# Four residual graph layers: edge counts by windows of 125 keys, with the first head's projection between the windows

## The reference

```
h = relu(layernorm(x));  x = x + GAT(h)    # layer 0 and 1: 4 heads of 512, elu, then 1 head of 768
h = relu(layernorm(x));  x = x + RGCN(h)   # layer 2: three convolutions over 3 relations
h = relu(layernorm(x));  x = x + GAT(h)    # layer 3: 8 heads of 96, elu, then 1 head of 768

GAT:  hW = h @ W                                     # per head
      e  = leaky_relu(as[src] + ad[dst], 0.2)        # for each edge, and for each node's loop to itself
      alpha = exp(e - max over the target's edges) / (their sum + 1e-16)
      out[dst] += alpha * hW[src];   out + b
RGCN: xw = h @ w_rel[r];  inv[dst, r] = 1 / (number of edges of type r into dst), 0 where there are none
      out[dst] += xw[edge_type, src] * inv[dst, edge_type];   out + h @ w_root + b;  relu
```

## Time and profile before

| | us |
|---|---|
| median of 3 runs | 1873.45 |
| lowest and highest | 1873.04, 1873.78 |
| the profiled execution | 1874.38 |
| its span | 1872.6 |
| PE, DVE, ACT, POOL busy | 1575.7, 880.6, 579.8, 517.1 |

### The profile page before, as it was taken

The page is one execution under the profiler, slowest core; times in us unless marked ns, Lnnn a source line. Parts: engine busy times, 40 slices in busy tenths (PEclk is TensorE's granted clock), DMA queues, the critical chain, the costliest instruction groups (busy, mean ns, idle before and its releaser), DMA issues.

```text
span 1872.6 us, 27057 instructions
## 1 busy us (share of the span) xinstructions
PE 1575.7 (84%) x10264; PEld 1515.3 (81%) x10264; DVE 880.6 (47%) x2103; ACT 579.8 (31%) x1165; POOL 517.1 (28%) x671
## 2 busy tenths in 40 slices
PE   3978888997779889976899999999999995566777
PEld 2647888896779888976899999999999995556777
DVE  4995566423356664233634223140322134678633
ACT  2114444332244343222231222322221222355421
POOL 1014233332242233313222332323232222222121
PEclk7998898997889899988899999999999997767797
DMA  1112111122221111223111122112122222100012
GB/s 50 38 37 69 45 46 45 35 67 77 66 64 33 40 46 34 80 69 110 39 39 42 50 64 64 54 49 62 49 68 82 75 85 71 38 1 1 5 47 86
DMA packets 85290, 99.24 MB, mean 53 GB/s; under 512 B 8742, under 2 KB 77788, under 8 KB 85166
## 3 DMA queue, kind: packets, MB, share of 16 engines
q1 hardware_dynamic: 68660, 66.50, 12.4%
q10 hardware_dynamic: 16506, 31.07, 5.1%
HBM read 85.76 MB, written 11.77 MB: 52 GB/s over the span
## 4 chain that ended last, share of the span: by engine, by line
PE 61%; DVE 11%; issue 10%; ACT 7%; DMA 6%; POOL 3%; DVEq 1%; ACTq 0%; POOLq 0%; SPq 0%
PE ps L705 35%; PE ps L768 7%; PE ps L871 6%; PE ps L853 4%; PE ps L735 3%; DMA xl<-x_scratch 2%; PE ps L830 2%; DVE prob L1693 2%; DVE junk L1646 2%; DMA xl<-in_x 1%; PE ps L892 1%; POOL pairs L966 1%; PE ps L915 1%; ACT pairs L1049 1%; DVE rl L1729 1%
## 5 line engine op out<-in xcount | busy, mean ns | idle before, releaser
L966 POOL TENSOR_TENSOR pairs<-stage,pairs 128x256 fp32r<-128x256 f32 (+3 forms) x472 | 370.0, 802 | 792.7 <-ACT pairs L1049 791.5
L705 PE MATMUL ps<-pairs,XB 128*125 128x256 f32 (+2 forms) x2880 | 416.4, 307 | 28.1 <-POOL pairs L966 17.0
L705 PEld LDWEIGHTS ps<-pairs,XB 128*125 128x125 f32 (+1 forms) x2880 | 409.5, 195 | 31.7 <-issue 18.0
L705 PE MATMUL ps<-pairs,XA 128*125 128x256 f32 (+3 forms) x2655 | 375.2, 303 | 1.1 <-DVE Hl L1354 1.1
L705 PEld LDWEIGHTS ps<-pairs,XA 128*125 128x125 f32 (+2 forms) x2655 | 370.6, 189 | 2.8 <-DVE Hl L1354 1.7
L1049 ACT ACTIVATE pairs<-stage 128x256 fp32r<-128x256 f32 (+3 forms) x472 | 188.9, 424 | 554.7 <-PE ps L705 426.4
L768 PE MATMUL ps<-AT,Hg 125*128 125x314 f32 (+1 forms) x1080 | 167.4, 316 | 15.3 <-ACT full L1107 7.9
L768 PEld LDWEIGHTS ps<-AT,Hg 125*128 125x128 f32 (+1 forms) x1080 | 161.8, 191 | 17.3 <-ACT full L1107 9.2
L1354 DVE TENSOR_TENSOR Hl<-ps,Hl 125x768 fp32r<-125x768 f32 (+3 forms) x57 | 43.6, 818 | 273.0 <-ACT Hl L1099 273.0
L735 PE MATMUL ps<-ident,prob 125*125 125x125 f32 x475 | 89.9, 348 | 82.3 <-ACT full L1107 35.6
L735 PEld LDWEIGHTS ps<-ident,prob 125*125 125x125 f32 x475 | 80.5, 254 | 88.3 <-issue 34.2
(11 more groups left out here) (196 smaller groups left out, 1706.3 us busy)
## 6 DMA issues: line engine op xcount, KB each, us to landing
stage<-in_W SPq DMA_DIRECT2D x192, 128.0 KB, 2.3
stage<-in_rel SPq DMA_DIRECT2D x99, 192.0 KB, 2.4
stage<-in_root SPq DMA_DIRECT2D x91, 64.0 KB, 1.8
x_scratch<-xo ACTq DMA_DIRECT2D x15, 375.0 KB
xl<-x_scratch ACTq DMA_DIRECT2D x15, 375.0 KB
stage<-in_rel SPq DMA_DIRECT2D x42, 128.0 KB, 2.1
stage<-in_root SPq DMA_DIRECT2D x12, 192.0 KB, 2.4
stage<-in_W SPq DMA_DIRECT2D x12, 192.0 KB, 2.4
```

The source lines that it names most:

```text
L705: last = mm(o, X[:rows, xi, a, P * (s0 + t):P * (s0 + t) + m], pair(n, b), start=k == 0 and i == 0 and t * pitch % BANK == 0, stop=k == le ...
L966: nc.gpsimd.tensor_tensor(pair(n, 1), staged(n), pair(n, 0).bitcast(F32), ALU.subtract).then_inc(*up("weights_lo", "weights lo", n))
```

## The change

In neutral words, part by part:

1. **Windows.** The key on the target side is now 3 x target + type, and the source alone the key on the other side. 1875 target keys make 15 windows of 125 (`NW`, `KW`). A chunk now costs a `srcs` of 626 keys and a `dsts` of 125, and 2 products of 313 columns into 2 banks. A group is 2 chunks (`EG` = 2), with 2 pairs of one-hot buffers. With these edges the 15 windows take 3, 4, 3, 4, 4, 4, 3, 4, 3, 4, 4, 3, 4, 4 and 3 passes: 54, so 108 chunks.
2. **The start.** `bounds` works on 16 windows and 40 groups: 32 transposes on PE and 15 additions in a row on DVE instead of 10 and 5, two reductions that must see both halves, and two more small operations. PE and DVE load their trip counts with one address load and 32, 31 register loads. All five `load_x` stand before all five `norm_T`.
3. **Regrouping.** A window's counts are one ACT copy (with one row sum), and SP writes them to DRAM. After every third window SP waits for the writes and reads 125 x 1875 counts back as `cr_back`, one row for each target. DVE's `sum_relations` works on that, and has 4 operations instead of 7; the absent pairs are found by POOL, the logarithm with the loops to itself by ACT in two operations (`log_self`).
4. **Order.** Behind each of the windows 0 to 11 stands one weight tile of head 0's projection (15 products); the rows of chunk 0 are copied at window 5, those of chunk 1 at window 11, the dots stand at windows 7 and 13, and the `graph` steps at windows 4, 7, 10, 13 and behind 14.
5. **Degrees and repeats.** The row sums stand as 125 x 15, are transposed by PE (`degree_T`), written to DRAM and read back as `cnt`. The `repeats` step stands behind the dots of head 1's first chunk.
6. **SP** loads weights only as far as the splits of the steps that it has passed.

```diff
-EG = 4
+EG = 2
+KW = 125
+NW = R * N // KW
+NB = 16
+SP2 = N + 1
...
     if l == 0:
-        yield ("repeats",)
...
+        for w in range(NW):
+            yield ("count", w)
+            if w < 12:
+                yield ("part", chunk(0, w // 6), w % 6, w % 6 + 1)
+                yield ("split", chunk(0, w // 6), w % 6 + 1)
+            if w in (5, 11):
+                yield ("rows", chunk(0, w // 6))
+            if w in (7, 13):
+                yield ("dots", chunk(0, w // 6 - 1 if w == 7 else 1))
+            if w % 3 == 1 and w > 3:
+                yield ("graph", w // 3 - 1)
+        yield ("graph", NT - 1)
...
             yield second
+            if l == 0 and h < 0:
+                yield ("degree_T",)
+                yield ("repeats",)
+            if l == 0 and h == 0:
+                yield ("inverse",)
...
-    for d in range(NT + 2):
-        if d < NT:
-            yield ("load_x", d)
-        if d > 1:
-            yield ("norm_T", 0, d - 2)
+    yield ("split", ("project", 0, 0, 256), 0)
     for d in range(NT):
-        yield ("count", d)
+        yield ("load_x", d)
+    for d in range(NT):
+        yield ("norm_T", 0, d)
...
-                    q = acquire(*s, banks=4)
-                    o = ps[:P, place[q] * BANK:(place[q] + 4) * BANK]
-                    for c in range(4):
-                        last = mm(o[:, BANK * c:BANK * c + BANK], zero16[:, :P], zero16[:, :], start=True,
+                    w = s[1]
+                    q = acquire(*s)
+                    o = halves(q, P, SP2 // 2)
+                    for c in range(2):
+                        last = mm(o[:, c, :], zero16[:, :P], zero16[:, :SP2 // 2], start=True,
...
+                            for c in range(2):
+                                last = mm(o[:, c, :], dsts[:, i, :KW],
+                                          srcs[:, i, SP2 // 2 * c:SP2 // 2 * c + SP2 // 2],
                                           start=False, stop=True, skip_group_check=True)
...
+                    sp.dma_start(cr_scr[KW * w:KW * w + KW, :], cr[:, w % 2, :N]).then_inc(
+                        *up(f"counts_out{w % 2}", "counts out", w, by=16))
+                    if w % 3 == 2:
+                        d = w // 3
+                        sp.wait_ge(*at("counts out", w))
+                        sp.wait_ge(*at("counts out", w - 1))
+                        sp.dma_start(cr_back[:, d, :].rearrange("p (r n) -> p r n", r=R),
+                                     cr_scr[R * P * d:R * P * d + R * P, :].rearrange("(p r) n -> p r n", r=R)).then_inc(
+                            *up(f"counts_back{d}", "counts back", d, by=16))
...
-                    load_weights(LOADS)
-                elif s in tiles_of:
-                    load_weights(wend[s] + 12)
+                parted = max(parted, split_limit(s))
+                load_weights(next((n for n in range(len(W)) if (stage_before[n] or 0) >= max(parted, 1)), len(W)))
...
+                elif kind == "graph":
+                    d = s[1]
+                    pool.wait_ge(*at("edge counts", d))
+                    nc.gpsimd.tensor_scalar(lnc[:, d, :N], cn[:, d % 2, :N], 0.0, ABSENT, ALU.is_equal,
+                                            ALU.mult).then_inc(*up("pool_step", "absent", False, d))
...
+                    log_mask(False, d, cw, 1 - d % 2)
...
-                    for d in range(NT):
-                        step(V.tensor_tensor(span[:, 2, d + 1:d + 2], span[:, 2, d:d + 1], span[:, 1, d:d + 1],
+                    for w in range(NW):
+                        step(V.tensor_tensor(span[:, 2, w + 1:w + 2], span[:, 2, w:w + 1], span[:, 1, w:w + 1],
                                              ALU.add))
...
-                            V.tensor_scalar(srcs[:, i, :], iota16[:P, :], edgef[:, 0, bass.ds(group * EG + i, 1)],
+                            V.tensor_scalar(srcs[:, i, :], iota16[:P, :SP2], edgef[:, 0, bass.ds(group * EG + i, 1)],
...
-                dve.wait_ge(*at("relation counts", d))
+                dve.wait_ge(*at("counts back", d))
                 if d >= 2:
                     dve.wait_ge(*at("graph out", d - 2))
+                    dve.wait_ge(*at("mask", False, d - 2))
```

More of the change, by code:

```diff
@@ L924, in _ @@
         def _(sp):
-            loaded = [0]
+            loaded, parted = [0], 0
             def load_weights(upto):
@@ L1559, in _ @@
                         dve.wait_ge(*at("edge keys"))
-                    with dve.Fori(passes[d], passes[d + 1]) as g:
-                        group = nc.s_assert_within(g + shift_of[d], 0, NG - 1, skip_runtime_bounds_check_because=
-                                                   "a pass's group lies between its tile's first and last")
+                    with dve.Fori(passes[w], passes[w + 1]) as g:
+                        group = nc.s_assert_within(g + shift_of[w], 0, NG - 1, skip_runtime_bounds_check_because=
+                                                   "a pass's group lies between its window's first and last")
```

272 lines of the change are left out of this document (146 added, 126 removed).

## The result

| us | before | changed |
|---|---|---|
| median | 1873.24 | 1896.13 |
| lowest and highest of 4 runs | 1871.70, 1873.78 | 1894.89, 1897.37 |
| the profiled execution, its span | 1874.38, 1872.6 | 1897.37, 1895.6 |
| first softmax row of head 0 | 177.77 | 198.20 |
| from there to the end | 1694.8 | 1697.4 |

The ratio is 1.0124 [1.0106, 1.0141]: slower by 22.9 us, where 1876.6 and a range of 1855 to 1893 were forecast. The spans differ by 23.0, and 20.4 of it have come by head 0's first softmax row. So the loss lies where the prediction looked, and is seven times as large.

What follows compares the result with a forecast made beforehand. DVE and PE were taken as nearly full in the counts. Terms put window 14's end at 161.6 and the first softmax row at 177.4, 0.4 earlier; repeats add 3.6, so 1873.45 + 3.2 gives 1876.6 us, range 1855 to 1893.

Steps and rivals of the forecast that it cites:

- 0.52 a chunk: Windows' loop: DVE needs 0.46 a chunk, hand-overs with two buffer pairs raise it to 0.52 us, at most 0.60.
- prepared chunks: Windows 1 to 12: two chunks DVE fills during projection; 1.3 us with zero products and the loop's end and start.
- The clock: Counts: low clock at the start and after four long waits adds 11.8 us, bounds 3 and 27.
- Rival 2: Windows: PE stays at the 1.2 GHz level in nine of windows 1 to 12; +15.7, 1892.3 us; chance 0.15.
- POOL: Windows: POOL's splits and mask work hold up DVE's one-hots, 10.5 us, bounds 4 and 22.
- Rival 3: Windows: POOL's work meets one-hots nearly always through shared ports; +11.6, 1888.2 us; chance 0.11.
- The waits for rows and dots: Counts: row copies at windows 5 and 11 cost 8.2 us, dots and sums at windows 7 and 13 cost 8.3.
- The first weights: Behind window 0: first split waits for ACT's copy, then ACT and POOL split; 2.1 us.
- The start: Up to the first one-hot: bounds ready near 15.3, norm ends 29.0, register reads 9.9; first one-hot at 38.9 us.
- The tail: Behind window 14 to the first softmax row: copy, DRAM trip, sums with mask, scores; 15.8 us, row at 177.4.
- the DRAM trip: Behind window 14: last counts written in 2.5 us and read back in 6.4, bounds together 6 and 12.
- The repeats: Head 1: DVE's repeats stand ahead of the low part, all 3.55 us counted on the path to its scores.

Runs made afterwards that it cites:

- e9: Changed kernel with two sets of two one-hot buffers, taken in turn by passes; 1875.66 us, ratio 1.0017 to the kernel before.
- e10: Changed kernel with head 0's whole projection moved behind the windows, plus four one-hot buffers; 1878.55 us, ratio 1.0025 to the kernel before.
- e15: e10 with each chunk's two products done a second time into a spare bank; 1877.30 us, ratio 1.0024 to the kernel before.
- e1: Changed kernel with head 0's whole projection moved behind the windows; 1885.05 us, ratio 1.0060 to the kernel before.
- e4: Changed kernel with POOL's three mask operations on one column for tiles 0 to 3; 1883.21 us, ratio 1.0068 to the kernel before.
- e2: Changed kernel with zero-row products added on PE ahead of windows 0, 6, 8, 12 and 14; 1905.38 us, ratio 1.0172 to the kernel before.
- e5: e1 with each chunk's two real products repeated into a spare bank; 1883.36 us, ratio 1.0056 to the kernel before.
- e8: Changed kernel with degree and repeats steps ahead of the projection of head 1's second chunk; 1909.96 us, ratio 1.0203 to the kernel before.

## Why the prediction was wrong

- **The step that failed** is "I take 0.52 a chunk, between 0.46 (DVE never waits) and 0.60". Measured: 0.63 at the high clock and 0.78 at the low one, both outside these ends. I had added DVE's work and a little; with two buffers the time of a pass is a loop through both engines, DVE's writing and PE's reading, and so it takes in PE's time at whatever clock. The 54 passes, added up window by window on PE, took some 82 us, where my terms held 50 for them (64 x 0.52, 24 prepared chunks of 0.26, 20 x 0.52). With some 9 for the low clock and 7.6 for POOL taken off, an estimate from the rows, the pace itself cost 16 more than forecast. e9 shows how much hangs on the buffers: with four of them the windows take 20.6 us less, and window 13 takes 4.68 instead of 5.97 at the same clock.
- **The clock** was in the sum with 11.8, and this term was too small as well. It was low for 98 us of 142, which cost 11.1 in the projection's parts (35.6 against 12 x 2.04) and 0.31 in each of some 30 low passes: about 20, 8 more than forecast. Rival 2 named this (nine windows low, 1892.3), its sign (a mean clock under 0.7) came true with 0.66, and it comes nearest to the result. But it had nothing for the hand-over. e10 and e15 show that with four buffers the counts take the same time at 0.67 and at 0.92; no run shows two buffers at a high clock with nothing added. Clock and hand-over feed each other: e1 shows a loop that never leaves the low level by itself.
- **POOL** was in with 10.5. One-hots lost 7.6 to it in the windows, of it 4.9 to the masks (forecast 4.8), so this term was not short. Without the masks the windows are 13 shorter (e4), more than twice what DVE lost to them directly; the rest came with shorter waits and a higher clock. The absent pairs take 2.45 on POOL, where I had put 1.0 without a row. Rival 3's sign, one-hots of 1 us and more in most windows, didn't come: there were three. I had also misread the counts before: they hold not one clash with POOL but three, the one of the earlier trace rows and

```profile
80.45 1.53 DVE L1568 TENSOR_SCALAR dsts<-iota,edgef 125x125 f16<-125x125 f16 x1
...
94.91 1.50 DVE L1568 TENSOR_SCALAR dsts<-iota,edgef 125x125 f16<-125x125 f16 x1
```

- **The waits for rows and dots**: 16.5 forecast, 15.2 measured. The first weights: 2.1 and 2.08. Both right.
- **The start**: register reads 9.9 forecast, 10.3 measured; but the bounds came at 17.4, not 15.3 (the edges' data came 1.3 later, and the transposes with their wait took 1.8 more where I had 1.1), and the norm ended at 31.7, not 29.0. So the first one-hot came 3.1 later than forecast.
- **The tail**: 15.8 forecast, 14.1 measured; the DRAM trip 8.8 against 8.9. The DRAM trip was late last, as said. **The repeats**: 3.6 on the path forecast, 2.6 to 4.3 measured.

The sum of the misses: start +3.1, windows +19.3 (142.0 against 122.7), tail -1.7, repeats -1.0, in all 19.7 against the 19.5 between forecast and median. (In rival 2 nine windows at 2.3 and 0.4 make 24.3, not 24.5; nothing hangs on it.)

## What to carry over

Before a loop between two engines is made finer, work out its pass as a ring, the way round of one buffer: one engine's time, the other's at its slow clock, and both hand-overs, divided by the number of buffers; only when that is below the slower engine's own time does the engine's time count. Put the loop's own branch and register work, here 0.3 a pass, into that engine's time. Halving the buffers together with the work of a step leaves no slack for the hand-overs, which don't shrink with the work. And work that is moved between the steps of a thin loop runs at that loop's clock: price it at the low level, here 3.56 instead of 2.04.

## What the runs showed of the hardware

- Products with a single row of zeros kept PE busy for 12.0 of 12.0 us with the clock at 0.50 (e2); whether the single row or the zeros matter wasn't tried. Doubling the products of 125 rows took the clock of the counts from 0.50 to 0.93 (e1, e5).
- 31 register reads and two address loads took 10.3 us on DVE: about 0.31 for a read, as much as for an address load.
- On POOL the comparison of 625 16-bit counts takes 2.45, an addition of 625 floats 1.50. Beside the addition that starts at 123.90 a one-hot took 1.23. Beside the comparison at 120.34 four one-hots took their usual 0.37 and 0.24, and beside the one at 88.79 a `dsts` took 0.74.
- The order of steps in layer 0 changed the time of the layers behind it by up to 14 us, 10.6 of it as longer products on PE (e8); the cause is open.
